# An attention and feed-forward layer on one core: store signals per slot, and a reordered feed-forward seam

## The reference

```python
q = x @ Wq.T                                # 32 heads of 128
k = rope(x @ Wkr.T) on rotary channels, (x @ Wdk.T) @ Wupk.T on the others
v = (x @ Wdk.T) @ Wupv.T                    # 8 heads, each used by 4 query heads
attn = softmax(where(causal, rope(q) @ k.T / sqrt(128), -1e9))
x1 = layernorm(x + (attn @ v) @ Wo.T)
W = unpack4(w) * s                          # byte = two signed 4-bit values, one scale per 64
x2 = layernorm(x1 + (silu(x1 @ W1.T) * (x1 @ W3.T)) @ W2.T)   # hidden width 1376
```

## Time and profile before

| | us |
|---|---|
| median of three runs | 2431.09 |
| the profiled execution | 2429.89 |
| its span (first to last instruction) | 2428.1 |
| PE busy | 2382.8 (98% of the span) |
| ACT busy | 1625.5 (67%) |
| DVE busy | 1440.9 (59%) |
| POOL busy | 573.0 (24%) |

### The profile page before, as it was taken

One profiled execution on the slowest core, in us unless ns is written; L12 is line 12 of the kernel. 1 busy time (PEld: TensorE's weight loads), 2 busy tenths in 40 slices (PEclk: granted clock), 3 DMA queues, 4 the chain that ended last, 5 costly groups with the idle time before them and its releaser, 6 DMA issues.

```text
span 2428.1 us, 40379 instructions
## 1 busy us (share of the span) xinstructions
PE 2382.8 (98%) x12028; PEld 1997.9 (82%) x12028; DVE 1440.9 (59%) x3752; ACT 1625.5 (67%) x3213; POOL 573.0 (24%) x441
## 2 busy tenths in 40 slices
PE   8999999999999999999999999999999998899998
PEld 7888888888888888888888888888888876778886
DVE  5334666666666666666666666666666677842332
ACT  4223878788887878787878878787878774422211
POOL 3002313232231313131322313132313203400000
PEclk9999999999999999999999999999999999999999
DMA  7867323334242323333332424232323325420100
GB/s 268 285 212 290 127 101 113 106 106 142 70 167 91 130 82 134 104 112 101 107 127 89 160 81 148 78 138 89 127 95 112 119 95 169 137 83 35 52 35 18
DMA packets 110934, 293.43 MB, mean 121 GB/s; under 512 B 10784, under 2 KB 27680, under 8 KB 101600
## 3 DMA queue, kind: packets, MB, share of 16 engines
q1 hardware_dynamic: 110880, 292.73, 35.8%
HBM read 208.80 MB, written 88.08 MB: 122 GB/s over the span
## 4 chain that ended last, share of the span: by engine, by line
PE 87%; DVE 4%; ACT 3%; issue 2%; DMA 2%; SPq 1%; POOL 0%; ACTq 0%; DVEq 0%; POOLq 0%
PE b_ps L260 41%; PE b_sps L260 31%; PE b_tps L1502 9%; PE b_tps L1552 2%; PE b_ps L1552 2%; PE b_tps L260 1%; ACT b_sc L964 1%; DVE c_sl L1242 1%; DMA c_sl<-in_s2p 1%; ACT b_pt L979 1%; DVE c_pk L1263 1%; ACT b_sc L958 1%; DVE b_qf L1188 0%; DVE c_pk L1253 0%; DMA b_xs<-xs_d 0%
## 5 line engine op out<-in xcount | busy, mean ns | idle before, releaser
L1217 DVE TENSOR_TENSOR b_pt<-b_tps,b_pt 128x512 fp32r<-128x512 f32 (+3 forms) x768 | 427.1, 556 | 304.5 <-ACT b_pt L979 299.4
L260 PE MATMUL b_sps<-b_kt,b_qs 128*128 128x512 f32 (+4 forms) x2304 | 497.5, 343 | 0.0
L979 ACT ACTIVATE b_pt<-b_tps 128x512 fp32r<-128x512 f32 (+3 forms) x768 | 368.5, 480 | 192.1 <-PE b_tps L1502 190.2
L260 PEld LDWEIGHTS b_sps<-b_kt,b_qs 128*128 128x128 f32 x2304 | 403.1, 188 | 54.4 <-issue 0.6
L260 PE MATMUL b_ps<-b_xs,b_wq 128*128 128x512 f32 x1536 | 441.0, 407 | 0.3 <-DMA b_xs<-xs_d 0.3
L964 ACT ACTIVATE b_sc<-b_sc,b_rinv 128x896 f32<-128x896 f32 (+7 forms) x512 | 396.0, 773 | 65.8 <-DVE b_rinv L1207 59.3
L260 PE MATMUL b_ps<-b_pt,b_vt 128*128 128x512 f32 x1584 | 434.8, 403 | 1.8 <-DVE b_ys L1228 1.2
L260 PE MATMUL b_ps<-b_wo,b_ot 128*128 128x512 f32 x1536 | 422.5, 405 | 1.2 <-DVE b_ys L1228 1.2
L958 ACT ACTIVATE b_sc<-b_sc,b_nmax 128x896 f32<-128x896 f32 (+7 forms) x512 | 394.9, 771 | 29.2 <-DVE b_nmax L1199 28.9
L1199 DVE CUSTOM_DVE_ANT_0 b_sc<-b_sps,b_mask 128x896 f32<-128x896 f32 (+7 forms) x512 | 386.7, 755 | 19.9 <-PE b_sps L260 19.8
L1502 PE MATMUL b_tps<-b_ident,b_sc 128*128 128x128 f32 x2304 | 375.5, 273 | 11.3 <-ACT b_sc L964 7.1
(11 more groups left out here) (137 smaller groups left out, 2282.6 us busy)
## 6 DMA issues: line engine op xcount, KB each, us to landing
b_xs<-xs_d SPq DMA_DIRECT2D x32, 2048.0 KB, 9.2
b_ys<-y_d SPq DMA_DIRECT2D x128, 256.0 KB, 2.6
y_d<-b_ys SPq DMA_DIRECT2D x128, 256.0 KB, 2.6
k_d<-a_ks SPq DMA_DIRECT2D x32, 512.0 KB, 4.0
v_d<-a_vs SPq DMA_DIRECT2D x32, 512.0 KB, 3.0
b_kt<-k_d SPq DMA_DIRECT2D x64, 256.0 KB, 4.4
b_vt<-v_d SPq DMA_DIRECT2D x16, 1024.0 KB, 4.8
b_wraw<-in_wqT SPq DMA_DIRECT2D x64, 256.0 KB, 2.7
```

The lines of the kernel that those rows point to most:

```text
L260: ins = nc.tensor.matmul(out, *every[n], start=(n == 0), stop=(n == len(every) - 1))
L979: nc.scalar.activation(pt[:, u % PT_UNITS, HI, 0:nj, h * P:(h + 1) * P], tps[n % 2][:, 0:nj], ACT.Copy)\
L1217: nc.vector.tensor_tensor(pt[:, u, LO, 0:nj, h * P:(h + 1) * P], tps[n % 2][:, 0:nj], pt[:, u, HI, 0:nj, h * P:(h + 1) * P], ALU.subtract) ...
```

## The change

- `a_k_out` becomes four semaphores, one for each slot of `a_ks`. ScalarE's rotary part n waits for the stores of slot n of the blocks before; its other part n waits for this block's rotary store of slot n alone.
- The down matrix's two shifts of 512 columns become four instructions of 128 columns, each doing both shifts with a shift amount per partition. The parts are renumbered: 3 is the shifts, 4 the multiply.
- "End" turn, VectorE: at step 0 the reciprocals of cells 30 and 31, then all of norm1's reciprocal root and tiles 0 and 1; at step 1 tiles 2 and 3. Before, the reciprocal of cell 31 stood at step 1 and norm1's work after the low parts of step 0.
- TensorE's three waits after the "end" turn (among them the last y sum) move to just before down 0, past up 1.
- SP: the loads of tile 3 move into step 11 of the "end" turn, ahead of the last store of y.
- The down matrix of tile 2: its unpacking moves from the "end" turn to after gate 0, its copy to after the high copy of hidden 0. In the first block ScalarE's copy of the down matrix of tile f+3 moves from iteration f to iteration f+1, behind the high copy of hidden f+1. In iteration 0 VectorE does the low part of hidden 0 before part 0 of tile 3.
- ScalarE's square root for the second block moves from iteration 7 to iteration 8.

```diff
+        ROOT = {"first": 8, "next": 2, "last": FT}
...
-                             words(a_ks[:, n % 4])).then_inc(a_k_out, 16)
+                             words(a_ks[:, n % 4])).then_inc(a_k_out[n % 4], 16)
...
+                    if turn == "end" and step == 11:
+                        c_weights(EARLY)
...
-            for f in range(EARLY, FT):
+            for f in range(EARLY + 1, FT):
                 c_weights(f)
                 if f == EARLY + 1:
                     c_store_x1(0)
...
             def a_rope_hi(t):
-                act.wait_ge(a_k_out, 16 * 8 * t + a_OUT0)
...
                 for n in range(4):
+                    if type(t) is not int or t:
+                        act.wait_ge(a_k_out[n], 16 * 2 * t)
...
             def a_nope_hi(t):
-                act.wait_ge(a_k_out, 16 * (8 * t + 4) + a_OUT0)
                 for n in range(4):
+                    act.wait_ge(a_k_out[n], 16 * (2 * t + 1))
...
                     c_hidden(n, index, what)
+                    if place == "first" and what + EARLY - 1 < FT:
+                        c_weights_hi(what + EARLY - 1, (2,))
                     if place == "first" and what + EARLY < FT:
-                        c_weights_hi(what + EARLY)
+                        c_weights_hi(what + EARLY, (0, 1))
...
-                    if what == NORM[place][1]:
+                    if what == ROOT[place]:
                         norm1.square_root(act, n + 1)
...
                     if turn == "end" and step == WO7:
-                        c_weights_hi(2)
+                        c_weights_hi(2, (0, 1))
...
                     elif part == 3:
-                        nc.vector.tensor_tensor(down, down, c_sh[0:n, 1:5, 0:1].broadcast_to((n, 4, P)),
-                                                ALU.logical_shift_left).then_inc(c_shifted, 1)
-                    elif part == 4:
-                        dve.wait_ge(c_shifted, 4 * f + 3)
-                        nc.vector.tensor_tensor(down, down, c_sh[0:n, 1:5, 1:2].broadcast_to((n, 4, P)),
-                                                ALU.arith_shift_right).then_inc(c_shifted, 1)
+                        for k in range(4):
+                            nc.vector.tensor_scalar(down[:, k], down[:, k], c_sh[0:n, 1 + k, 0:1],
+                                                    c_sh[0:n, 1 + k, 1:2], ALU.logical_shift_left,
+                                                    ALU.arith_shift_right).then_inc(c_shifted, 1)
...
+                    if place == "first" and what == 0:
+                        c_unpack(EARLY - 1, (3, 4))
-                    if ahead:
+                    if ahead and what:
                         c_unpack(ahead, (0,))
                     c_hidden_lo(n, what)
                     if ahead:
-                        c_unpack(ahead, (1, 2, 3, 4, 5))
+                        c_unpack(ahead, (1, 2, 3, 4) if what else range(5))
...
-                    if cell := cell_at(step - 2, it, turn):
+                    if turn == "end" and step == 0:
+                        for c in (CELLS - 2, CELLS - 1):
+                            reciprocal(LAST, c)
+                        norm1.reciprocal_root(dve, 0)
+                        norm1.scale_tiles((0, 1))
+                    elif turn != "end" and (cell := cell_at(step - 2, it, turn)):
                         reciprocal(*cell)
...
-                    if turn == "end" and step == 0:
-                        norm1.reciprocal_root(dve, 0)
-                    if turn == "end" and step < 2:
-                        norm1.scale_tiles((2 * step, 2 * step + 1))
+                    if turn == "end" and step == 1:
+                        norm1.scale_tiles((2, 3))
...
                     if turn == "end" and step == WO7 - 1:
-                        c_unpack(1, (3, 4, 5))
+                        c_unpack(1, (3, 4))
                     if turn == "end" and step == WO7:
-                        c_unpack(2, range(6))
+                        c_unpack(2, (0, 1, 2))
...
             def c_down(n, f):
+                if type(n) is int and n == 0 and f == 0:
+                    pe.wait_ge(pt_lo, PIECES * GROUPS + PTLO0)
+                    pe.wait_ge(ot_lo, QT * GROUPS)
+                    pe.wait_ge(y_added, QT * GROUPS)
...
             turns(pe, turn_of)
-            pe.wait_ge(pt_lo, PIECES * GROUPS + PTLO0)
-            pe.wait_ge(ot_lo, QT * GROUPS)
-            pe.wait_ge(y_added, QT * GROUPS)
```

More of the change, by code:

```diff
@@ L405, in layer @@
         a_kr_lo = sem("a_kr_lo")
-        a_k_out, a_xs_out, a_y_out = sem("a_k_out"), sem("a_xs_out"), sem("a_y_out")
+        a_k_out = [sem(f"a_k_out{n}") for n in range(4)]
+        a_xs_out, a_y_out = sem("a_xs_out"), sem("a_y_out")
         a_v_out = [sem("a_v_out0"), sem("a_v_out1")]
@@ L722, in _ @@
             sp.wait_ge(a_wd_lo, 2)
-            sp.wait_ge(a_k_out, 16 * 8 * 2 + a_OUT0)
+            for slot in range(4):
+                sp.wait_ge(a_k_out[slot], 16 * 2 * 2)
             load_k(0)
@@ L748, in _ @@
             sp.wait_ge(a_xs_out, 16 * NBLK + a_OUT0)
-            sp.wait_ge(a_k_out, 16 * 8 * NBLK + a_OUT0)
+            for slot in range(4):
+                sp.wait_ge(a_k_out[slot], 16 * 2 * NBLK)
             for p in range(2):
@@ L858, in _ @@
             act.sem_inc(a_xs_out, a_OUT0)
-            act.sem_inc(a_k_out, a_OUT0)
             act.sem_inc(a_v_out[0], a_OUT0)
@@ L936, in hi_q @@
                 if type(it) is int and it == 0 and blk == 1:
-                    act.wait_ge(a_k_out, 16 * 8 * NBLK + a_OUT0)
+                    for slot in range(4):
+                        act.wait_ge(a_k_out[slot], 16 * 2 * NBLK)
                 nc.scalar.activation(qs[:, blk, h, HI], qf[:], ACT.Copy).then_inc(q_hi, 1)
@@ L1255, in c_unpack @@
                     elif part in (1, 2):
-                        dve.wait_ge(c_shifted, 4 * f + part)
+                        dve.wait_ge(c_shifted, 6 * f + part)
                         c_multiply(f, part - 1, P, DC * n)
                     elif part == 3:
-                        nc.vector.tensor_tensor(down, down, c_sh[0:n, 1:5, 0:1].broadcast_to((n, 4, P)),
-                                                ALU.logical_shift_left).then_inc(c_shifted, 1)
-                    elif part == 4:
-                        dve.wait_ge(c_shifted, 4 * f + 3)
-                        nc.vector.tensor_tensor(down, down, c_sh[0:n, 1:5, 1:2].broadcast_to((n, 4, P)),
-                                                ALU.arith_shift_right).then_inc(c_shifted, 1)
+                        for k in range(4):
+                            nc.vector.tensor_scalar(down[:, k], down[:, k], c_sh[0:n, 1 + k, 0:1],
+                                                    c_sh[0:n, 1 + k, 1:2], ALU.logical_shift_left,
+                                                    ALU.arith_shift_right).then_inc(c_shifted, 1)
                     else:
-                        dve.wait_ge(c_shifted, 4 * f + 4)
+                        dve.wait_ge(c_shifted, 6 * f + 6)
                         c_multiply(f, 2, n, D)
@@ L1376, in turn_of @@
                         norm1.variance(dve, 0)
-                    if turn == "last" and 26 <= step:
+                    if turn == "last" and 26 <= step < 31:
                         if step == 26:
```

## The result

The changed kernel takes 2442.81 us (median of 6 runs, 2439.33 to 2444.1), the kernel before 2433.00 beside it (2430.56 to 2436.87): a ratio of 1.0037, 95% interval 1.0027 to 1.0047. I had forecast 2409.5, faster. The profiled execution has 2444.1 us and a span of 2442.3, 14.2 more than before.

A forecast was written before the change was run, and what follows sets the result against it. PE, busy 98% of the span, was taken as the bound, so gains come only from idle and low-clock stretches. Terms sum to -21.3, adjusted to -21.6: profiled 2429.89 becomes 2408.3, predicted median 2409.5 us, range 2402 to 2419.

The forecast's parts named there:

- Iterations 2 to 7: First block: freed Silu and quicker shifts cut losses from 6.5 to 3.4 us despite later buffers; minus 3.1 us.
- Stage A: PE's thirteenth group starts 4.9 us earlier through per-slot signals, and 1.7 us of low clock goes; minus 6.6 us.
- End of the attention: Earlier reciprocal and norm1 tiles shrink two PE pauses and remove low clock, less shift and low-part costs; minus 3.2 us.
- y sum: Before up 1: PE's 2.09 us wait for the last y sum is covered, with 1.7 low clock; minus 3.8 us.
- down 0: First block: hidden 0's low part comes first, removing a 2.9 us pause and 1.7 us of low clock; minus 4.6.
- Down 1: First block: new 3.3 us wait for hidden 1's low part behind tile 4's loads, plus 1.7 low clock; plus 5.0.
- Iteration 8: First block: with the root moved, down 8's loss of 3.25 us and 1.7 us of low clock goes; minus 5.0.
- Signs of being wrong: Narrow shifts over 0.4 us each, iterations staying above 9.2 us, or pauses of iterations 1 and 2 over 5 us each.
- lock: First block: each narrow shift can wait for a GpSimd instruction; about 3 us more, 2412.5 us; chance 0.15.
- Buffer: First block: later-freed load buffers make loads hold hidden's low part; up to 25 us more, 2434 us; chance 0.07.

The follow-up runs named there:

- e1: The changed kernel with the four waits for the key stores asked once, not four times, before the first q of the first turn: 2422.72 us.
- e2: The kernel before with 11 more ScalarE instructions (satisfied waits) ahead of the attention loop: 2450.07 us, ratio 1.0074.
- e6: e1 with ScalarE's copy of the down matrix of tile f+3 back in iteration f, ahead of Silu f+1: 2418.87 us.
- e12: e1 with no deferred copy, tile 2 unpacked whole at the last wo group, x1's store behind tile 4's loads, next y's load behind tile 8: 2416.71 us.
- e4: The kernel before with only the key stores' signals per slot, asked once before the first q: 2425.66 us, ratio 0.9975.
- e5: e1 with the down matrix's two shifts of 512 columns back in place of four of 128: 2425.09 us.
- e14: e12 with the down copy between Silu and hidden's high copy, and norm1's chain and first tiles back behind VectorE's step 0 jobs: 2413.6 us.
- e16: e14 with the two shifts of 512 columns instead of four narrow ones: 2414.63 us, ratio 0.9924.
- e7: e1 with the low part of hidden ahead of VectorE's shifts of the next tile in every iteration: 2421.2 us.

## Why the prediction was wrong

By starts of rows, changed against before: up to the first transposes in the fence of the result +14.2 (by ScalarE's branches stage A -6.2, the loop's 13 turns +20.3), from there to pv 7 -1.0, to down 0 -7.0, the first block +8.0, behind it 0.0; together the 14.2 of the spans. The forecast was -21.6. Of the 35.8 us between them the loop has 20.3, the first block 12.8 and the end of the attention 2.2. Two steps failed, then: without the first, in e1, the time is 2422.72 us, still above my range (2402 to 2419), mainly by the second.

- *The step that failed most is one that isn't in the sum:* the attention loop. I read that it has almost no idle time and that no edit stands in it, and took it at 0; it is +20.3 (e1, e2). The page showed 23 instruction packets on its queue, the trace has none of them in the loop, and I never asked what kept them out. The per-slot signals were priced at the waits that they remove on ScalarE, not at the instructions that they add.
- *Iterations 2 to 7, -3.1:* the second step, +7.6 and in e1 +7.0. A two-iteration chain of loads should take 16.8 to 17.2 us; by the issues of tiles 6, 8 and 10 in e1 (2057.71, 2079.23, 2101.31) it takes 21.5 and 22.1. The deferred copy holds the buffer longer than I gave it (e6: 4.3 us of the block, with six iterations still 3.3 us longer than before). Four narrow shifts take 3.1 to 4.3 us instead of 0.97, which was right only where GpSimd rests (1.10). The loads of tile 5 I put behind the store of x1 and its wait at 7.5 us; that was 8.8 in e1, and the pause 3.16 us and not 2.0 (3.54 in the changed kernel; e12: 4.3 us of the block).
- *Stage A, -6.6:* right, -6.2, and -6.3 by e4's medians. The clock came back as said.
- *End of the attention, -3.2:* mis-sized, -1.0. "In return the low part of cell 29 waits, 0.3 to 0.6 us" failed (and the sum had it at 0.2): norm1's chain waits 0.77 us for ScalarE's root and then stands in GpSimd's time, so this low part comes 2.3 us later than before, counted from the transposes at 2015.76. PE waits 0.96 us for it, 1.97 in e6, where pv 6 ran at the full clock. The narrow shifts there are not it: with the wide pair (e5) the stretch is 18.1 us as well. And the reciprocal ahead did not take away the pause of 1.62 us: in e14 it is 1.56, as the next low part then stands behind norm1's tiles.
- *y sum -3.8 and down 0 -4.6:* right. Of these 8.4 us, 1.7 is the half clock behind down 0's start; 6.7 stand ahead of it, and that was 7.0. Neither has a pause.
- *Down 1, +5.0:* right. The wait came, 4.53 us and half a clock behind. From down 0 to down 1 it was 9.90 us before, with that half clock in it, and 12.85 after: +2.95, where +5.0 and -1.7 make +3.3.
- *Iteration 8, -5.0:* right in kind: no pause and no half clock before down 8. The stretch from down 7 on is 2.6 us shorter and not 5.0 (in e1 3.4), as it now begins with the half clock behind down 7's new pause.
- *Signs of being wrong:* two of the three came, narrow shifts of over 0.4 us each (3.1 us for four is 0.78) and iterations above 9.2 us (62.95 us for the six from down 1 to down 7).
- *Rivals:* "lock" was true as a mechanism, though it costs the wide pair as much (e16). "Buffer" was the right one for the block's sign, at a smaller price than 25. None had the code's place.

## What to carry to other kernels

A hand-written loop on one engine has a place in its code as well as a length: before comparing two versions, look at the instruction queue's packets and at "issue" pauses behind a branch, and try the same kernel with a few satisfied waits more or fewer ahead of it. Count an edit's instructions on an engine even where they cost no time. When VectorE's work is moved, ask whether GpSimd is at work at the new place; and keep a load that waits for a store's landing out of a queue that feeds a double buffer.

## What the runs showed of the hardware that I had not expected

- ScalarE's code comes in packets of 8 KB. A loop of 320 issued instructions ran from what it held at the places 345, 350, 440 and 478, and was fetched five times a turn at 356, 396 and 484. It cost 1.3 to 1.6 us a turn on average at 356 and 484, and 0.3 us at 396.
- A VectorE instruction on 4 columns took 0.16 us, and 1.20 beside GpSimd (e6). Four of 128 columns took 1.10 us alone, and 3.1 to 4.3 beside GpSimd (e1).
- A half clock that falls ahead of a wait for another engine cost nothing here: pv 6's 21 products took 6.56 us in e7 and 5.07 in e6, and the next transposes stood at 2007.04 and 2007.05 us.
- From the issue of x1's store of 1 MB to that of the y load that waits for it, 7.7 to 9.1 us passed in the kernels that start from the changed one, and 10.2 to 11.6 in the kernel before, e4 and e2.
